# Inverse standard deviation of the layer-norm tails: a power on GpSimd in place of a square root on ScalarE and a reciprocal on VectorE

## The reference

```python
def _layernorm(x, axis=-1, eps=1e-05):
    m = jnp.mean(x, axis=axis, keepdims=True)
    v = jnp.var(x, axis=axis, keepdims=True)
    return (x - m) / jnp.sqrt(v + eps)

x = _layernorm(x + _L0_attn_ref(x, ...))   # gated feed-forward and a series
x = _layernorm(x + _L0_ffn_ref(x, ...))    # product with a LoRA mixture
x = _layernorm(x + _L1_attn_ref(x, ...))   # attention over one key: a product
x = _layernorm(x + _L1_ffn_ref(x, ...))    # quantised gated feed-forward
x = _layernorm(x + _L2_attn_ref(x, ...))   # four layers of a scan and an MLP
x = _layernorm(x + _L2_ffn_ref(x, ...))    # product with two LoRAs
x = _layernorm(x + _L3_attn_ref(x, ...))   # attention, 32 heads, one key head
x = _layernorm(x + _L3_ffn_ref(x, ...))    # quantised gated feed-forward
```

## Time and profile before

| | |
|---|---|
| three timed runs | 1482.77, 1483.90, 1485.15 us, median 1483.9 |
| profiled execution, its own time | 1478.49 us |
| its span, first to last instruction | 1476.7 us |
| mean granted TensorE clock | 0.913 |
| TensorE busy | 1282.8 us (87%) |
| VectorE busy | 749.6 us (51%) |
| ScalarE busy | 426.7 us (29%) |
| GpSimd busy | 143.8 us (10%) |
| transfers | 78.82 MB, mean 53 GB/s |

### The profile page before, as it was taken

The page is one execution under the profiler, slowest core; times in us unless marked ns, Lnnn a source line. Parts: engine busy times, 40 slices in busy tenths (PEclk is TensorE's granted clock), DMA queues, the critical chain, the costliest instruction groups (busy, mean ns, idle before and its releaser), DMA issues. The chain is left out here.

```text
span 1476.7 us, 14587 instructions
## 1 busy us (share of the span) xinstructions
PE 1282.8 (87%) x5314; PEld 844.3 (57%) x5314; DVE 749.6 (51%) x1301; ACT 426.7 (29%) x709; POOL 143.8 (10%) x208
## 2 busy tenths in 40 slices
PE   7999997859699998982655789899999999699998
PEld 4787665324388887762443345554555443388877
DVE  5223323792655555324565564567778670333254
ACT  2222111110222114210222113244555567412141
POOL 0000000490000000001111013021111010000000
PEclk9999998889899999985666699889999999899999
DMA  7110001550065630004000000000000000021000
GB/s 305 43 43 0 0 0 70 200 193 0 28 229 195 231 129 0 1 17 139 1 0 0 0 22 22 2 2 2 1 2 0 2 2 1 25 82 64 21 21 37
DMA packets 18681, 78.82 MB, mean 53 GB/s; under 512 B 3330, under 2 KB 4226, under 8 KB 16452
## 3 DMA queue, kind: packets, MB, share of 16 engines
q1 hardware_dynamic: 18628, 78.13, 14.7%
HBM read 75.76 MB, written 2.10 MB: 53 GB/s over the span
## 5 line engine op out<-in xcount | busy, mean ns | idle before, releaser
L346 PE MATMUL psum<-L_ffn_x,L_ffn_w_up 128*128 128x512 f32 x1200 | 276.2, 393 | 16.2 <-DVE L_ffn_x L475 16.2
L346 PEld LDWEIGHTS psum<-L_ffn_x,L_ffn_w_up 128*128 128x128 f32 x1200 | 227.8, 190 | 64.3 <-issue 16.6
L1739 DVE TENSOR_REDUCE mqa_top<-psum 128x1 f32<-128x512 f32 (+3 forms) x304 | 181.6, 655 | 54.8 <-PE psum L1560 27.9
L1655 ACT ACTIVATE mqa_prob<-psum 128x512 f32<-128x512 f32 x288 | 161.4, 600 | 122.8 <-PE psum L1575 121.3
L363 PE MATMUL psum<-L_ffn_wd,L_ffn_part_h 128*128 128x512 f32 x600 | 141.7, 397 | 7.0 <-DVE L_ffn_wd L298 7.0
L1575 PE MATMUL psum<-mqa_stack,mqa_keys 100*128 100x512 f32 x288 | 130.2, 478 | 12.2 <-DMA mqa_stack<-mqa_rows 9.4
L363 PEld LDWEIGHTS psum<-L_ffn_wd,L_ffn_part_h 128*128 128x128 f32 x600 | 114.2, 192 | 31.7 <-DVE L_ffn_part_h L289 7.8
L1554 PE MATMUL psum<-mqa_keys,mqa_stack 96*128 96x512 f32 (+3 forms) x384 | 124.9, 391 | 2.1 <-DVE mqa_stack L1713 0.9
L346 PE MATMUL psum<-L_attn_x,L_attn_w_up 128*128 128x512 f32 x480 | 111.3, 394 | 3.9 <-DVE L_attn_hidden L464 3.9
L346 PEld LDWEIGHTS psum<-L_attn_x,L_attn_w_up 128*128 128x128 f32 x480 | 91.2, 190 | 23.8 <-issue 4.8
L1575 PEld LDWEIGHTS psum<-mqa_stack,mqa_keys 100*128 100x128 f32 x288 | 54.4, 196 | 88.1 <-ACT mqa_prob L1655 54.1
(11 more groups left out here) (237 smaller groups left out, 1593.5 us busy)
## 6 DMA issues: line engine op xcount, KB each, us to landing
L_ffn_stage<-in_L_w SPq DMA_DIRECT2D x25, 768.0 KB, 6.5
L_ffn_z_int<-in_L_z SPq DMA_DIRECT2D x14, 768.0 KB, 4.4
L_ffn_s_all<-in_L_s SPq DMA_DIRECT2D x14, 768.0 KB, 6.2
lora_wo<-in_L_wo SPq DMA_DIRECT2D x8, 1024.0 KB, 4.8
L_attn_stage<-in_L_w SPq DMA_DIRECT2D x10, 512.0 KB, 3.6
L_attn_w_down<-in_L_down SPq DMA_DIRECT2D x1, 2560.0 KB, 24.4
x_feat<-in_x_feat SPq DMA_DIRECT2D x2, 1024.0 KB, 7.1
x_tok<-in_x_tok SPq DMA_DIRECT2D x1, 2048.0 KB, 18.8
```

The source lines that it names most:

```text
L346: ins = nc.tensor.matmul(bank[half][:, :], w_up[:, slot, w_part, at:at + P], x[:, x_part, k, half * HALF:(half + 1) * HALF], start=k == 0 ...
L1655: nc.scalar.activation(prob[:, n % PROBS, :], score_bank[n % 3], ACT.Exp, scale=SCALE)\
L1739: nc.vector.tensor_reduce(top[:, i % 2, lo // HALF, heads[0]:heads[-1] + 1], max_bank[n % 3][:, 0:len(heads) * width] .rearrange("p (h k) ...
```

## The change

Every tail takes its inverse deviation from GpSimd, in `Tail.pool`: an addition of eps and a power with the exponent -0.5 for each tile, with one semaphore between them (`var_eps`) and one to VectorE (`rstd_ready`). The square root on ScalarE and the reciprocal on VectorE are removed. `Tail.pool` is called in every block that has a tail, at the end of what GpSimd does there; in `lora_then_single_key` for both tails after the rotation. The exponent becomes a constant that is set once. Line numbers of the change are its own.

```diff
--- before.py
+++ after.py
@@ -67,12 +67,13 @@
 
 
 
-    NAMES = ("out_ready", "out_taken", "ln_step", "var_ready", "std_ready", "normed", "transposed", "feat_ready")
+    NAMES = ("out_ready", "out_taken", "ln_step", "var_ready", "var_eps", "rstd_ready", "normed", "transposed",
+             "feat_ready")
 
     def __init__(self, chip, out_bank, tr_bank, last=False):
         self.c, self.out_bank, self.tr_bank, self.last = chip, out_bank, tr_bank, last
 
-        (self.out_ready, self.out_taken, self.ln_step, self.var_ready, self.std_ready, self.normed,
+        (self.out_ready, self.out_taken, self.ln_step, self.var_ready, self.var_eps, self.rstd_ready, self.normed,
          self.transposed, self.feat_ready) = chip.tail_sems
         self.base = NT * chip.tails
         chip.tails += 1
@@ -97,16 +98,19 @@
             step(nc.vector.tensor_tensor(row, row, bias[:, :], ALU.add))
         step(nc.vector.bn_stats(c.stats[:, t, :], row))
         nc.vector.bn_aggr(c.mean_var[:, t, :], c.stats[:, t, :]).then_inc(self.var_ready, 1)
-        dve.wait_ge(self.std_ready, self.base + t + 1)
-        step(nc.vector.reciprocal(c.rstd[:, t:t + 1], c.std[:, t:t + 1]))
+        dve.wait_ge(self.rstd_ready, self.base + t + 1)
         nc.vector.tensor_scalar(row, row, c.mean_var[:, t, 0:1], c.rstd[:, t:t + 1],
                                 ALU.subtract, ALU.mult).then_inc(self.normed, 1)
 
-    def act_std(self, act, t):
+    def pool(self, pool):
         c, nc = self.c, self.c.nc
-        act.wait_ge(self.var_ready, self.base + t + 1)
-        nc.scalar.activation(c.std[:, t:t + 1], c.mean_var[:, t, 1:2], ACT.Sqrt,
-                             bias=c.eps[:, 0:1]).then_inc(self.std_ready, 1)
+        for t in range(NT):
+            pool.wait_ge(self.var_ready, self.base + t + 1)
+            nc.gpsimd.tensor_tensor(c.std[:, t:t + 1], c.mean_var[:, t, 1:2], c.eps[:, 0:1], ALU.add)\
+                .then_inc(self.var_eps, 1)
+            pool.wait_ge(self.var_eps, self.base + t + 1)
+            nc.gpsimd.tensor_tensor(c.rstd[:, t:t + 1], c.std[:, t:t + 1], c.half_power[:, :], ALU.pow)\
+                .then_inc(self.rstd_ready, 1)
 
     def act_copy(self, act, t):
         c, nc = self.c, self.c.nc
@@ -115,9 +119,8 @@
         nc.scalar.copy(c.x_feat[:, :, t * P:(t + 1) * P], src).then_inc(self.feat_ready, 1)
 
     def act(self, act):
-        for t in range(NT):
-            self.act_std(act, t)
-            if t and not self.last:
+        for t in range(1, NT):
+            if not self.last:
                 self.act_copy(act, t - 1)
         if not self.last:
             self.act_copy(act, NT - 1)
@@ -152,13 +155,14 @@
 def setup(c):
 
     nc = c.nc
-    c.eps = c.sb("eps", [P, 1], F32)
+    c.eps, c.half_power = c.sb("eps", [P, 1], F32), c.sb("half_power", [P, 1], F32)
     ready, zeroed = c.sem("const_ready"), c.sem("ident_zeroed")
     with nc.Block() as block:
 
         @block.gpsimd
         def _(pool):
             nc.gpsimd.memset(c.eps[:, :], EPS)
+            nc.gpsimd.memset(c.half_power[:, :], -0.5)
             nc.gpsimd.memset(c.ident[:, :], 0.0).then_inc(zeroed, 1)
             pool.wait_ge(zeroed, 1)
             nc.gpsimd.affine_select(out=c.ident[:, :], in_=c.ident[:, :], compare_op=ALU.not_equal, fill=1.0,
@@ -325,6 +329,10 @@
                         sp.wait_ge(tail.normed, tail.base + t + 1)
                         sp.dma_start(last[t], c.x_tok[:, t, :]).then_inc(stored, 16)
                     sp.wait_ge(stored, 16 * NT)
+
+            @block.gpsimd
+            def _(pool):
+                tail.pool(pool)
 
             @block.tensor
             def _(pe):
@@ -418,7 +426,6 @@
                 for t in range(NT):
                     if t + 1 < NT:
                         split_h(act, t + 1, 1, 0)
-                    tail.act_std(act, t)
                     if t + 2 < NT:
                         split_h(act, t + 2, 0, 0)
                     if t and not tail.last:
@@ -675,6 +682,8 @@
             def _(pool):
                 nc.gpsimd.memset(ones[:, :], 1.0).then_inc(ones_ready, 1)
                 c.rot.pool(pool)
+                tail.pool(pool)
+                tail_values.pool(pool)
 
             @block.tensor
             def _(pe):
@@ -1399,7 +1413,6 @@
         k_full, head_rows = sb("k_full", [P, TOK]), sb("head_rows", [P, 2])
         v = sb("v", [P, NT, 2 * HD])
         ident_b, hide_k = sb("ident_b", [P, P], BF16), sb("hide_k", [P, 4, P], BF16)
-        half_power = sb("half_power", [P, 1])
         top, shift = sb("top", [P, 2, 2, HEADS]), sb("shift", [P, 2, 2, 2, PAIRS], F32R)
         both = sb("both", [P, HEADS])
         rows = sb("rows", [4 * PAIRS, 2, P], F32R)
@@ -1451,7 +1464,6 @@
 
             @block.gpsimd
             def _(pool):
-                nc.gpsimd.memset(half_power[:, :], -0.5)
                 nc.gpsimd.memset(ident_b[:, :], 0.0)
                 nc.gpsimd.memset(hide_k[:, :, :], 0.0).then_inc(const, 1)
                 pool.wait_ge(const, 1)
@@ -1486,7 +1498,7 @@
                         nc.gpsimd.tensor_tensor(c.std[:, qt:qt + 1], c.mean_var[:, qt, 1:2], c.eps[:, 0:1], ALU.add)\
                             .then_inc(pool_step, 1)
                         pool.wait_ge(pool_step, i + 1)
-                        nc.gpsimd.tensor_tensor(c.rstd[:, qt:qt + 1], c.std[:, qt:qt + 1], half_power[:, :], ALU.pow)\
+                        nc.gpsimd.tensor_tensor(c.rstd[:, qt:qt + 1], c.std[:, qt:qt + 1], c.half_power[:, :], ALU.pow)\
                             .then_inc(std_ready, 1)
 
             @block.tensor
```

## The result

The change made the kernel slower by 26.5 us: 1510.98 us (1509.73 to 1512.75, four runs) against 1484.53 (1482.77 to 1486.35, four runs), ratio 1.0182, 95% interval 1.0166 to 1.0197. A second comparison gave 1512.18 against 1481.14, ratio 1.0206 (1.0165 to 1.0248), +31.0 us; one execution in each of its two groups (1583.44 and 4344.45 us) was in the slow state and is left out. The forecast was 1514.8 us and +30.9, in the range 1506 to 1525.

A forecast was written before the change was run, and what follows sets the result against it. The prediction took the latency from variance to VectorE's normalisation as what counts, with GpSimd's rotation ahead of the first LoRA tail. 22.6 + 8.3 = +30.9 us on 1483.9 gave 1514.8 us, range 1506 to 1525.

The forecast's parts named there:

- The queue on GpSimd: First LoRA tail: tile 0 waits for the rotation's end at 325.6, its normalisation coming 40.3 us later.
- Rival (3): GpSimd's queue does not bind, as if the tail were served in between; only latency counts, 1495.2 us; chance 0.05.
- The relief of GpSimd: First LoRA tail: with VectorE stopped, 9.2 us of disturbance go and the rotation ends at 325.6, not 334.8.
- Rivals (1): The rotation keeps its recorded pace, its spans being its own and not disturbance: 1524.0 us; chance 0.13.
- (2): Strict lock: everything VectorE held comes back to GpSimd, 8.0 us less, 1506.8 us; chance 0.09.
- The relief of VectorE: First LoRA tail after the rotation: VectorE undisturbed, tile 0 to end of tile 6 normalisation 29.9 us, before 46.2.
- The merge: Merge of wo and wv on TensorE: 23.9 us later, less 1.3 of cold start, +22.6 us.
- Latency: Variance to normalisation 1.12 us a tile instead of 0.74, d = +0.38; short tails together +8.3 us.
- The table loads: ScalarE: six of 14 table loads go, under cover, put at 0, with -7.7 us (6 x 1.28) as far bound.
- (4) faster: Table loads and ScalarE's queue were on the path, no stall in the first LoRA tail: 1476.2 us; chance 0.02.
- (5) a dearer pair: The pair on GpSimd costs 0.56 us more each time: about +15 in all, 1530 us; chance 0.05.
- the prediction's lower bound: First LoRA tail: every port-using VectorE microsecond, 17.2 us, lost to GpSimd comes back, 8.0 us under the sum.

The follow-up runs named there:

- after_no_rot: Changed kernel (pair on GpSimd in all tails) with the rotation's ten doublings left out: 1469.12 us, ratio 0.9924 to the kernel before.
- after_paused: Changed kernel, GpSimd reordered: seven doublings, first LoRA tail's pairs, wait for the wo sums, last three doublings, values tail: 1484.11 us, ratio 1.0003 to the kernel before.
- lora_on_pool: Kernel before with only the first LoRA tail on GpSimd, the six others keeping square root and reciprocal: 1504.20 us, ratio 1.0175.
- extra_l1: Changed kernel with two more powers before each tile's own in the L1 feed-forward tail: 1520.44 us, ratio 1.0242 to the kernel before.
- inter: Changed kernel with the first LoRA tail's pairs for tiles 0 to 6 placed between the rotation's instructions: 1498.45 us, ratio 1.0134 to the kernel before.
- extra_values: Changed kernel with one more power before each tile's own in the values tail: 1511.75 us, ratio 1.0189 to the kernel before.

## Why the prediction was right, point by point

- **The queue on GpSimd** (forecast: the tail's first addition directly behind the rotation, near 326): it starts at 327.96, as the last instruction ends, and 2.9 us of the 327.96 are the later start of the tail. From the first variance to that normalisation took 40.4 us in place of 0.74, forecast 40.3 later, measured 39.7. That it is the queue, and not the pair, is shown by after_no_rot and after_paused, which have the pair everywhere and not the loss. Rival (3), 1495.2, falls with it.
- **The relief of GpSimd** (forecast 9.2 us, rotation ends at 325.6 from a start at 284.98, 40.6): the rotation took 40.3 us, 287.68 to 327.98, where it had taken 49.8. Rivals (1), nothing relieved, and (2), 17.2 relieved, both fall; the multiplies of 2048 elements take 3.60 us for 3.62 and the addition 4.49 for 4.50.
- **The relief of VectorE** (forecast 29.9 us from the first normalisation to the end of that of tile 6): 30.3. The 0.4 more are a product of TensorE that I hadn't looked at: see the last section. The kernel without the rotation shows the size of this relief from the other side, 18.9 us.
- **The merge** (forecast +23.9 - 1.3): +23.4 - 1.2 = +22.2 for 22.6, twice; +21.4 in lora_on_pool, whose product of tile 2 took 4.74 us and held nobody up.
- **Latency** (d = +0.38): the pair takes 1.12 us from aggregate to normalisation in all tails. L1 +3.0 as forecast, and extra_l1 shows that it answers to latency at full rate; values +0.45 for 0.4. Convolution +2.2 for 2.5: I took 0.27 us off at two of its eight tiles, but those two are 3.01 us apart before and after, so they absorb all of it. Two LoRAs +1.3 for 1.6: the seven distances grew by 0.29, 0.07 and then 0, 0.26, 0, 0.26 and 0.02, so that TensorE takes part of it back every second tile; I had put 0.38 at the first and 0.14 at each. All six: 7.8 for 8.3.
- **The table loads**, put at 0: the number was wrong, the term right. The program has 14 load instructions, but the one of the convolution (L1168) stands in a loop and runs four times: before executes 17 loads and after 8, so nine went and not six, and the far bound should have been -11.5 us (9 x 1.28). None of the nine shows on the path. In the five tails with a load, aggregate to normalisation is 0.74 us in tile 0 as in the others; and the stretch with the convolution's four loads (last normalisation of L1 to the next variance) is 161.8 us with them and 161.9 without. Where a load did lie on the path, in lora_on_pool, it cost 1.28 us at its tile. The kernel with six tails changed has 9 loads in place of 17. By the figure of the Trainium skill ("ScalarE: Activation LUTs", section "What ACT_TABLE_LOAD costs"), 2.66 us a switch, eight loads on the path would be 21 us, as an estimate, and this kernel would have come out faster than the one before; it is slower. That figure counts a drain of 1.38 us beside the load's 1.28; in lora_on_pool, where ScalarE had been idle ahead of the load, the square root starts 0.02 us after the load's end and no drain shows.
- **The level.** 1510.98 for 1514.8: 3.8 us below. The slowdown is 4.4 below the forecast (26.5 for 30.9), and the median before moved up by 0.6, from 1483.9 to 1484.53, with a fourth run. Of the 4.4, 0.9 are in the sum (30.0 by the traces). 2.7 are a term that the prediction doesn't have at all: the start of the attention, where nothing but a constant was changed, is that much shorter, and TensorE runs there at the higher of its clocks for longer (last section). 0.8 are left. The second comparison has +31.0, near the forecast, but by the same account it should be 27.3. The intervals of the two, 24.6 to 29.2 us and 24.4 to 36.7, overlap, and what moves the value between them stays open.
- **Time alone would not have decided.** The first comparison's +26.5 us lies midway between the forecast's +30.9 and rival (2)'s +22.9. That the forecast's account is the right one rests on the rows above and on the experiments.

The rivals that held prices beyond this, (4) faster and (5) a dearer pair, show nowhere: the pair takes 0.19 + 0.57 us even directly behind the rotation.

## What to carry to other kernels

An operation that is cheap on a new engine costs what stands ahead of it there: read the program order of the engine that receives it at each place where it is called, and ask when the last instruction ahead of it ends, not how busy the engine is on average (GpSimd was at 10%). A longer latency is paid only where the next engine already waits at the end of the chain, and there once a tile. And look at background work that nobody waits for: here the rotation cost the kernel before 19 us through VectorE, and one wait that moved its last three doublings under a stage in which VectorE rests made that kernel 16.7 us faster.

## What the runs showed of the hardware beyond the forecast

**GpSimd and VectorE take turns.** I had costed the disturbance by averages. The rows of inter show its form: VectorE's instruction ends 0.3 to 1.1 us after the one of GpSimd that was there first, and GpSimd's next one has begun by then, in front of VectorE's next. So a short operation of VectorE costs about as much as the one of GpSimd beside it (3.81, 4.62 and 4.87 us beside 3.60, 3.66 and 5.36). It holds for the sums of wo, with two inputs in SBUF, and for the normalisation, a tensor-scalar operation (3.81 us in place of 0.55). The residual add, with one input in PSUM and one in SBUF, takes 0.67 us in the middle of it. Kernel before, VectorE:

```profile
316.55 0.67 DVE L92 TENSOR_TENSOR x_tok<-x_tok,psum 128x512 f32<-128x512 f32 x1
...
323.85 3.97 DVE L777 TENSOR_TENSOR lora_wo_sum<-lora_pair 128x512 f32<-128x512 f32 x1
```

The Trainium skill ("SBUF — State Buffer", section "Who interferes with whom") says that the pair of ports goes to whoever issues first, for the whole instruction, and that operations with two inputs in SBUF, or tensor-scalar operations in a two-port mode, take it; these rows agree. Read as the prediction's lower bound read it, every such microsecond of VectorE lost to GpSimd, it would have given 17.2 us of relief, and 9.5 were measured (49.8 - 40.3).

**A cold TensorE.** After 39 us with 0.37 us of work, TensorE starts at the lower of its two clocks. Stretches of after (columns as above, the granted clock the third from the end):

```profile
329.40:332.00 2.60, 2.57 (x6) 1.58 (x7) 2.53 (x4) 0.58 (x1) 0.00 (x0) 0.50 0.39 50
332.00:334.00 2.00, 2.00 (x4) 0.92 (x3) 1.03 (x3) 0.00 (x0) 0.74 (x2) 0.50 0.79 324
```

Before:

```profile
332.50:335.00 2.50, 2.48 (x6) 1.58 (x7) 2.43 (x4) 0.00 (x0) 2.03 (x4) 0.50 0.00 0
...
337.00:342.00 5.00, 5.00 (x16) 2.38 (x15) 1.80 (x2) 0.00 (x0) 0.00 (x0) 1.00 0.00 0
```

The product of tile 2, which had a granted clock of 0.50 (1.2 GHz) for some five of its microseconds, took 6.15 us; the next, at 1.00 (2.4 GHz), 3.60. TensorE wasn't the bound there, so of these 2.55 us only 0.41 reached VectorE, as its wait before the residual add of tile 2. In the kernel before the same cold start fell on the merge, after a gap of 9 us, and was paid in full, 1.2 us. A stall costs its clock penalty where the work behind it is the bound, and next to nothing where it isn't.

**A term that no forecast had.** From the last normalisation of the two-LoRA tail to the first of the attention it is 111.2 us in four of the five traces with the square root in that tail and 112.0 in the fifth (lora_on_pool). With the pair it is 108.3 to 108.6 in seven traces of eight, and 110.7 in the eighth, extra_values. The ten microseconds that begin 80 us after that normalisation tell them apart. Before, after and extra_values (columns as above):

```profile
959.40:969.40 10.00, 10.00 (x40) 5.48 (x38) 5.68 (x12) 3.56 (x7) 2.23 (x4) 0.50 0.01 3
991.60:1001.60 10.00, 9.95 (x53) 4.74 (x52) 5.72 (x14) 5.35 (x11) 2.44 (x4) 0.87 0.01 3
991.80:1001.80 10.00, 10.00 (x40) 5.59 (x36) 6.03 (x13) 3.21 (x6) 1.87 (x4) 0.50 0.01 3
```

With TensorE busy all the time, it starts 40 matmuls at a granted clock of 0.50 and 53 at 0.87. All six traces with 0.50 here have the longer stretch, all seven with 0.83 to 0.87 the shorter one. In the five microseconds ahead of these ten TensorE has gaps in both kernels (busy 3.12 us of 5 in before, 3.13 in after). extra_values has the pair in all tails like after, so it isn't the pair as such that decides; what in the order of work ahead does, these runs don't show. A kernel can gain or lose 3 us of 1480 in a stage that nobody touched.
